# The gates' stage taken into the recurrent mixer's stage

## What is computed

```python
h = h + _L0_attn_ref(_layernorm(h), W_qkv, conv_w, W_z, W_b, W_a, dt_bias, A_log, ...)
# inside it
mixed = hidden_states @ W_qkv.T                      # 2048 channels
y = depthwise_conv(mixed, conv_w)                    # 4 taps along the sequence
mixed = silu(y)                                      # q, k: 8 heads of 64; v: 16 heads of 64
beta = sigmoid(hidden_states @ W_b.T)                # 16 gates
g = -exp(A_log) * softplus(hidden_states @ W_a.T + dt_bias)   # 16 decays
# then, row by row: S = S*exp(g); delta = (v - S k)*beta; S += k delta; o = S q
```

## Time and profile before

| | |
|---|---|
| median of 3 runs | 2748.21 us (2746.57 to 2750.3) |
| profiled execution | 2751.68 us, span 2750.0 us |
| mean granted TensorE clock | 0.924 |
| TensorE, VectorE, ScalarE, GpSimd busy over the span | 2363.9, 1981.4, 1304.2, 839.3 us |
| gates' stage | 671.8 to 736.2 |
| first pair's projection and convolution | 736.3 to 777.7 |
| first pair's own turn, up to the next pair's products | 777.7 to 832.4 |

### The profile page before, as it was taken

The page is one execution under the profiler, slowest core; times in us unless marked ns, Lnnn a source line. Parts: engine busy times, 40 slices in busy tenths (PEclk is TensorE's granted clock), DMA queues, the critical chain, the costliest instruction groups (busy, mean ns, idle before and its releaser), DMA issues. The chain is left out here.

```text
span 2750.0 us, 53589 instructions
## 1 busy us (share of the span) xinstructions
PE 2363.9 (86%) x19286; PEld 1813.9 (66%) x19286; DVE 1981.4 (72%) x4757; ACT 1304.2 (47%) x3127; POOL 839.3 (31%) x698
## 2 busy tenths in 40 slices
PE   7999998997747998889899989878487958799998
PEld 6777776885725777777777777756374845577654
DVE  4898984333368898988888888897755436787772
ACT  0444443211256777767676777774130214455232
POOL 2111100000113333333333333334876037560110
PEclk9999998998568999999999999998778977899999
DMA  4221001001412221111122222233221862220000
GB/s 158 75 76 29 14 10 51 23 24 44 156 24 51 54 53 46 45 49 50 41 51 53 52 56 55 55 82 83 77 46 25 295 188 75 73 62 1 8 21 28
DMA packets 274614, 169.24 MB, mean 62 GB/s; under 512 B 182863, under 2 KB 250590, under 8 KB 274000
## 3 DMA queue, kind: packets, MB, share of 16 engines
q1 hardware_dynamic: 248221, 140.55, 18.0%
q0 software_dynamic: 26112, 25.03, 3.5%
HBM read 99.49 MB, written 73.45 MB: 63 GB/s over the span
## 5 line engine op out<-in xcount | busy, mean ns | idle before, releaser
L1405 POOL TENSOR_TENSOR qd<-decay,qm 114x456 f32<-114x456 f32 x128 | 162.0, 1285 | 551.8 <-DVE qm L1604 464.3
L2358 PEld LDWEIGHTS d_ps<-d_xT,resid 128*128 128x128 f32 x1024 | 198.0, 195 | 47.1 <-issue 29.7
L2358 PE MATMUL d_ps<-d_xT,resid 128*128 128x228 f32 x1024 | 216.5, 363 | 12.3 <-DMA d_xT<-normed_t 12.3
L1585 DVE TENSOR_TENSOR ue<-ue,elim_tmp 128x30 f32<-128x30 f32 (+14 forms) x480 | 210.2, 438 | 16.8
L3028 POOL DMA_INDIRECT s_eo<-rows_y,slots_all x128 | 153.2, 1197 | 147.4 <-POOLq L2795 109.4
L1583 DVE TENSOR_TENSOR elim_tmp<-ue 128x30 f32<-128x30 f32 (+14 forms) x480 | 178.6, 372 | 25.2 <-issue 9.8
L1647 DVE SCALAR_TENSOR_TENSOR y_v<-raw,taps,y_v 128x228 f32<-128x228 f32 x384 | 163.4, 498 | 45.0 <-ACT y_v L2025 45.0
L1987 ACT ACTIVATE decay<-d_ps,gates 114x114 f32<-114x114 f32 x512 | 137.9, 362 | 83.7 <-DVE nt L1617 48.6
L1647 DVE SCALAR_TENSOR_TENSOR y_qk<-raw,taps,y_qk 128x228 f32<-128x228 f32 x384 | 146.5, 455 | 23.3 <-ACT y_qk L2025 23.3
L1998 ACT ACTIVATE gl<-upto,gates 114x114 f32<-114x114 f32 x512 | 156.1, 392 | 0.5 <-PE d_ps L2346 0.2
L2334 PE MATMUL d_ps<-y_qk 64*114 64x228 f32 x512 | 73.8, 411 | 95.6 <-DVE nt L1617 57.0
(11 more groups left out here) (370 smaller groups left out, 5698.9 us busy)
## 6 DMA issues: line engine op xcount, KB each, us to landing
rows_x<-zero_row SPq DMA_DIRECT2D x4, 2048.0 KB
ue<-blocks_n SPq DMA_DIRECT2D x16, 512.0 KB, 5.1
blocks_u<-ue SPq DMA_DIRECT2D x16, 512.0 KB, 3.0
blocks_v<-on SPq DMA_DIRECT2D x16, 512.0 KB, 3.1
e_x<-rows_x SPq DMA_DIRECT2D x32, 256.0 KB, 4.5
e_gu<-L_ffn_w_gate_up SPq DMA_DIRECT2D x32, 256.0 KB, 4.6
rows_y<-e_y SPq DMA_DIRECT2D x32, 256.0 KB, 3.8
blocks_n<-nt SPq DMA_DIRECT2D x96, 64.0 KB
```

What stands on the lines that cost most here:

```text
L1405: pool.tensor_tensor(qd[p.par][s][:, hs(u), :].rearrange("p (a o b) t -> p a o b t", o=2, b=2)[:, :, o], e[o][:, :, :].rearrange("p (a b) ...
L1585: step = dve.tensor_tensor(ue[:, 0:j, j + 1:], ue[:, 0:j, j + 1:], part, ALU.subtract)
L2358: last = pe.matmul(ps[:, f % 2, (t % 2) * W:(t % 2 + 1) * W], w_qkv[:, k, t * 128:(t + 1) * 128], xT[:, k, :], start=(k == 0), stop=(k == ...
```

## The change

`prepare` is removed as a stage and its work moves into the block of `delta_net`, with `first_turns`. The group's functions (statistics, scaling, gate read, turn, gate product, copy, store) stay as they were; their buffers are now tiles of the mixer that are not yet in use (`upd` and `sz` for the four loads, `qd1` for the scaled rows, `on` for the columns, `nt1` for the softplus), and their banks are 2 to 5 for the turns and 6 and 7 for the gate products, so that banks 0 and 1 are free for projections.

The first pair (`p`) is projected and convolved between the groups, each engine's order written out by hand. SP loads the mixer's weights ahead of every store and of the loads of groups 4 to 7, and the first pair's columns once the store of group 0 has landed. The tile of gates is finished in two halves of 16 samples: the first after group 3's gate read, the second inside the first pair's own turn. VectorE's statistics, power and scaling of a group follow each other directly. The first pair's turn is that of `iteration(Pair(0, 0))`, with the second half of the gates put in.

Cut to its core:

```diff
-def prepare(c, hid, xts, gates, w_qkv, taps, qmask):
...
-c.stage(prepare, hid, xts, gates, w_qkv, taps, qmask)
...
-def first_turns(iteration, between=None):
-
-iteration(Pair(0, -1), a=False, z=False, d=False)
-if between:
-    between()
-iteration(Pair(0, 0), z=False, d=False)
-iteration(Pair(0, 1), d=False)
-iteration(Pair(0, 2))
-iteration(Pair(0, 3))
 
...
+    load_group(0)
...
+    for g in range(1, GB):
+        load_group(g)
+    sp.dma_start(w_qkv[:, :, :], dr["L0_attn_W_qkv_t"].rearrange("(k p) n -> p k n", p=128)).then_inc(mix_in, 16)
+    sp.dma_start(taps[:, :, :], dr["L0_attn_conv_w_c"]).then_inc(mix_in, 16)
+    c.clear_old(sp)
+    store_group(0)
+    load_group(4)
+    store_group(1)
+    load_group(5)
+    sp.wait_ge(xT_out[0], 16)
     load_x(Pair(0, 0))
+    store_group(2)
+    load_group(6)
+    store_group(3)
+    load_group(7)
     sp.dma_start(nd.rearrange("s h q j i -> (s h q) (j i)").rearrange("p (a d) -> p a d", d=D),
                  c.zero_row[:, :].unsqueeze(1).to_broadcast([128, 4, D])).then_inc(nd_zero, 16)
     sp.dma_start(w_z[:, :, :], dr["L0_attn_W_z_t"].rearrange("(k p) n -> p k n", p=128)).then_inc(wz_in, 16)
+    for g in range(FIRST, GROUPS):
+        store_group(g)
+    iteration(Pair(0, -1), a=False, z=False, d=False)
...
+    pool.memset(raw[:, :, :, 0:TAPS - 1], 0.0).then_inc(d_init, 1)
+    group_power(0)
+    group_power(1)
+    group_power(2)
+    group_power(3)
+    for s in range(2):
+        pool.memset(ut[s][:, :, :], 0.0).then_inc(d_init, 1)
+        pool.memset(zs[s][:, :, :], 0.0).then_inc(d_init, 1)
+    group_power(4)
...
+    def coefficients():
+        ch.note(dve.tensor_scalar(qmask[:, :], c.upto[:, :], -DH ** -0.5, None, ALU.mult))
+        dve.wait_ge(g_coef, 1)
+        ch.note(dve.tensor_scalar(coef[:, 0:H], coef[:, 0:H], -1.0, None, ALU.mult))
+        ch.note(dve.memset(coef[:, H:], -1.0))
+        ch.sync()
+    def positive(q):
+        dve.wait_ge(g_abs, q + 1)
+        ch(dve.tensor_scalar(gates[:, g_half(q), :], gates[:, g_half(q), :], 0.0, None, ALU.max))
+    def log_gates(q):
+        half = gates[:, g_half(q), :]
+        dve.wait_ge(g_exp, 2 * q + 2)
+        ch(dve.tensor_tensor(half, half, g_soft[:, g_half(q), :], ALU.add))
+        ch(dve.tensor_tensor(half, half, coef[:, :].unsqueeze(1).to_broadcast([S, B // 2, 2 * H]), ALU.mult))
+        dve.tensor_scalar(half, half, LOG_ZERO, None, ALU.max).then_inc(gates_r, 1)
+    p, nxt = Pair(0, 0), Pair(0, 1)
+    stat(0)
+    scale(0)
+    stat(1)
+    scale(1)
+    stat(2)
+    scale(2)
+    gate_read(0)
+    stat(3)
+    scale(3)
+    gate_read(1)
+    stat(4)
+    gate_read(2)
+    scale(4)
+    dve.wait_ge(mix_in, 32)
+    dve.tensor_scalar(taps[:, :, :], taps[:, :, :], 0.5, None, ALU.mult).then_inc(taps_r, 1)
+    dve.wait_ge(taps_r, 1)
+    gate_read(3)
+    coefficients()
+    positive(0)
+    stat(5)
+    scale(5)
+    conv(p, 0, 1)
+    conv(p, 0, 2)
+    conv(p, 0, 3)
+    log_gates(0)
+    gate_read(4)
+    stat(6)
+    scale(6)
+    conv(p, 1, 1)
+    conv(p, 1, 2)
+    conv(p, 1, 3)
+    gate_read(5)
+    stat(7)
+    scale(7)
+    conv(p, 2, 1)
+    conv(p, 2, 2)
+    conv(p, 2, 3)
+    gate_read(6)
+    silu(p, 0)
+    conv(p, 3, 1)
+    conv(p, 3, 2)
+    conv(p, 3, 3)
+    gate_read(7)
+    silu(p, 1)
+    ch.end()
+    scale_gate()
+    query_mask(p, 0)
+    weights(p, 0)
+    weights(p, 1)
+    query_mask(p, 1)
+    weights(p, 2)
+    weights(p, 3)
+    weights(p, 4)
+    query_mask(p, 2)
+    weights(p, 5)
+    query_mask(p, 3)
+    positive(1)
+    conv(nxt, 0, 1)
+    conv(nxt, 0, 2)
+    conv(nxt, 0, 3)
+    weights(p, 6)
+    weights(p, 7)
+    conv(nxt, 1, 1)
+    conv(nxt, 1, 2)
+    conv(nxt, 1, 3)
+    conv(nxt, 2, 1)
+    conv(nxt, 2, 2)
+    conv(nxt, 2, 3)
+    log_gates(1)
+    conv(nxt, 3, 1)
+    conv(nxt, 3, 2)
+    conv(nxt, 3, 3)
+    silu(nxt, 0)
+    silu(nxt, 1)
+    ch.end()
+    for n in range(2):
+        dve.wait_ge(xT_out[n], 16 * (GROUPS // 2))
...
+    def softplus(q):
+        soft = g_soft[:, g_half(q), :]
+        act.wait_ge(ab_read, 2 * GROUPS // 2 * (q + 1))
+        act.activation(soft, gates[:, g_half(q), :], ACT.Abs).then_inc(g_abs, 1)
+        act.wait_ge(g_abs, q + 1)
+        act.activation(soft, soft, ACT.Exp, scale=-1.0).then_inc(g_exp, 1)
+        act.wait_ge(g_exp, 2 * q + 1)
+        act.activation(soft, soft, ACT.Ln, bias=1.0).then_inc(g_exp, 1)
+    p, nxt = Pair(0, 0), Pair(0, 1)
+    group_read(0)
+    group_read(1)
+    act.wait_ge(gw_in, 64)
+    act.activation(coef[:, 0:H], coef[:, 0:H], ACT.Exp).then_inc(g_coef, 1)
+    group_read(2)
+    group_read(3)
+    raw_read(p, 0)
+    raw_read(p, 1)
+    act.wait_ge(taps_r, 1)
+    softplus(0)
+    group_read(4)
+    raw_read(p, 2)
+    raw_read(p, 3)
+    first_tap(p, 0)
+    raw_read(p, 4)
+    raw_read(p, 5)
+    group_read(5)
+    first_tap(p, 1)
+    raw_read(p, 6)
+    raw_read(p, 7)
+    group_read(6)
+    first_tap(p, 2)
+    first_tap(p, 3)
+    tanh(p, 0)
+    act.wait_ge(gates_r, 1)
+    decay_terms(p, 0)
+    group_read(7)
+    decay_terms(p, 1)
+    tanh(p, 1)
+    decay_exp(p, 0)
+    decay_terms(p, 2)
+    decay_exp(p, 1)
+    decay_terms(p, 3)
+    raw_read(nxt, 0)
+    raw_read(nxt, 1)
+    raw_read(nxt, 2)
+    raw_read(nxt, 3)
+    raw_read(nxt, 4)
+    decay_exp(p, 2)
+    raw_read(nxt, 5)
+    raw_read(nxt, 6)
+    decay_terms(p, 4)
+    decay_exp(p, 3)
+    raw_read(nxt, 7)
+    decay_terms(p, 5)
+    decay_exp(p, 4)
+    decay_terms(p, 6)
+    decay_terms(p, 7)
+    decay_exp(p, 5)
+    softplus(1)
+    decay_terms(nxt, 0)
+    first_tap(nxt, 0)
+    first_tap(nxt, 1)
+    decay_exp(p, 6)
+    decay_exp(p, 7)
+    first_tap(nxt, 2)
+    first_tap(nxt, 3)
+    tanh(nxt, 0)
+    tanh(nxt, 1)
+    decay_terms(nxt, 1)
+    act.wait_ge(gates_r, 2)
...
+    p, nxt = Pair(0, 0), Pair(0, 1)
+    turn_group(0)
+    turn_group(1)
+    group_gates(0)
+    turn_group(2)
+    group_gates(1)
+    turn_group(3)
+    group_gates(2)
+    pe.wait_ge(mix_in, 32)
+    project(p, 0)
+    project(p, 1)
+    group_gates(3)
+    turn_group(4)
+    project(p, 2)
+    project(p, 3)
+    turn_group(5)
+    group_gates(4)
+    project(p, 4)
+    project(p, 5)
+    turn_group(6)
+    group_gates(5)
+    project(p, 6)
+    project(p, 7)
+    turn_group(7)
+    group_gates(6)
+    group_gates(7)
+    decay(p, 0)
+    products(p, 0)
+    decay(p, 1)
+    project(nxt, 0)
...
```

More of the change, by code:

```diff
@@ new lines, in scale @@
+                def scale(g):
+                    dve.wait_ge(grstd, g + 1)
+                    if g >= 2:
+                        dve.wait_ge(g_t, 2 * (g - 1))
+                    for s in range(GS):
+                        last = dve.tensor_scalar(g_xn[g % 2][:, s, :], g_hs[g % GB][:, s, :], g_mv[g % 2][:, s, 0:1],
+                                                 g_rstd[g % 2][:, s:s + 1], ALU.subtract, ALU.mult)
+                        if s < GS - 1:
+                            ch.note(last)
+                    ch.sync()
+                    last.then_inc(gxn, 1)
@@ L1971, in _ @@
+                iteration(Pair(0, 3))
                 with dve.Fori(0, LOOPS) as j:
@@ L2761, in last_turns, with turn_group @@
                         down(g)
-                first_turns(iteration)
+                def turn_group(g):
+                    pe.wait_ge(gxn, g + 1)
+                    if g >= 2:
+                        pe.wait_ge(gxT, g - 1)
+                    bank = 2 + 2 * (g % 2)
+                    for k in range(KD):
+                        for s in range(GS):
+                            last = pe.transpose(ps[:, bank + k, s * S:(s + 1) * S], g_xn[g % 2][:, s, k * 128:(k + 1) * 128],
+                                                c.ident[0:S, 0:S])
+                        last.then_inc(g_t, 1)
@@ new lines, in group_gates @@
+                def group_gates(g):
+                    if g == 0:
+                        pe.wait_ge(gw_in, 64)
+                    pe.wait_ge(gxT, g + 1)
+                    if g >= 2:
+                        pe.wait_ge(ab_read, 2 * (g - 1))
+                    for s in range(GS):
+                        for k in range(KD):
+                            last = pe.matmul(ps[0:S, 6 + g % 2, s * 2 * H:(s + 1) * 2 * H], g_xT[g % 2][:, k, s * S:(s + 1) * S],
+                                             w_ab[:, k, :], start=(k == 0), stop=(k == KD - 1))
+                    last.then_inc(ab_mm, 1)
@@ new lines, in _ @@
+                project(nxt, 3)
+                project(nxt, 4)
+                decay(p, 3)
+                project(nxt, 5)
+                products(p, 1)
+                project(nxt, 6)
+                decay(p, 4)
+                project(nxt, 7)
+                decay(p, 5)
+                products(p, 2)
+                decay(p, 6)
+                products(p, 3)
+                decay(p, 7)
+                iteration(Pair(0, 1), d=False)
+                iteration(Pair(0, 2))
+                iteration(Pair(0, 3))
```

248 lines of the change are left out of this document (87 added, 161 removed).

## The result

| | before | changed |
|---|---|---|
| median, measured together | 2749.75 us (2746.57 to 2753.1, 5 runs) | 2734.46 us (2731.95 to 2736.64, 5 runs) |
| the same pair measured again later | 2753.69 us (2747.32 to 2754.6, 9 runs) | 2729.3 us (2727.97 to 2739.54, 5 runs) |
| profiled execution, span | 2750.0 us | 2733.0 us |

The account below looks back on a forecast made before the run. Bound: two stretches in sequence, 106 us with 53.5 us of work on the busiest engine, refilled as load queue and engine orders allow. Gain 17.6 (middle of 20.3 and 14.9) less 1.0, taken as 16: 2732 us, range 2722 to 2745.

Parts of the forecast that it names:

- Step 1, the queue: Load queue ahead of the first projection: 6.07 MB at 177 GB/s, first pair's columns landing at 707, bounds 701 to 714.
- Step 2: Up to the first half of the gates: two projections done at 713, group 3's gate product at 714.6 to 716.1.
- The new order's worst stall: VectorE, idle since about 707, waits some 8 us to read group 3's gates, which stands in front of group 5's statistics.
- Steps 3 and 4: First pair and hand-over: first products at 756 or 762, second pair's first raw read at 763.2 or 768.6, gain 20.3 or 14.9.
- the high column: Timetable with TensorE's clock high for the middle pairs of projections: first tile 726.8, silus 752.4 and 760.8; low: 729.9, 757.9, 766.2.
- Step 5: Gates' second half inside the first pair's turn, covered by VectorE's wait for GpSimd's mask: costs 1 us, 3.4 without that cover.
- the prediction's own sign: Step 5 is wrong if VectorE does not wait for the mask, or second pair's first taps slip by over 2 us.
- Nothing downstream should give the gain back.: Behind the second pair's turn the kernel is unchanged and each turn follows the one before, so the gain should stay.
- (a): Rival: overlap mostly in name, first columns land behind the last group at 716 to 718; gain 6, 2742 us; chance 0.09.
- (b): Rival: TensorE's clock stays low through the first pair's turn too, costing 8.4 us of 14; 2743 us; chance 0.11.
- (d): Rival: slower, first columns land late, at 737 behind 9.4 MB at the lowest queue rate; 2762 us; chance 0.06.
- (c): Rival: hand-overs hide, weights at 304 GB/s, columns at 703, clock high in all pairs; gain some 24, 2724 us; chance 0.06.

## Why the prediction came out

The number was right: 16 us forecast, 15.3 and 24.4 between the medians, 19.0 at the first elimination. Step by step:

- **Step 1, the queue.** Columns at 707 forecast, in use at 708.58: right within its bounds. The copy on the chip confirms that this landing held the first projection (2.9 us).
- **Step 2.** Gate read of group 3 at 714.6 to 716.1 behind a stall of some 8 us: 716.25, 8.67 us. Place and size right. "The new order's worst stall" was wrong in weight: with the stall cut to 1.96 us the raw read moved by 1.0.
- **Steps 3 and 4.** First products at 756 or 762: 757.58. First raw read at 763.2 or 768.6: 763.37, the gain of 20.3 rather than the middle taken. VectorE met the high column within 1 us (first tile done at 727.7 for 726.8, first silu at 753.0 for 752.4, second at 761.3 for 760.8), yet the clock was not high in every pair: the four pairs of projections took 6.04, 3.26, 6.20 and 4.72 us at granted clocks of 0.54, 1.00, 0.53 and 0.70. In the second profile of the change the third pair took 4.64, and the raw read came no earlier (91.6 against 91.4). So the clock did not choose between the columns, as the prediction had it.
- **Step 5.** One microsecond forecast; 20.3 became 19.0, and leaving the half out gave 1.2 back. Size right, mechanism not: the sum took the 2.67 us of waiting for the mask as a cover that stays. The mask moved instead: 10.07 us became 3.24, and VectorE's own end decides; by the prediction's own sign the step was wrong. The first taps slipped by 1.2 us against the turn (from 24.8 to 26.1 us behind the raw read), where 1.8 was forecast. On the table loads the row held: in the change the load for the logarithm starts at 718.01 and takes 1.28, the function starts at 719.31.

```profile
718.01 1.28 ACT L2355 ACT_TABLE_LOAD   x1
719.31 0.63 ACT L2355 ACTIVATE nt<-nt 114x512 f32<-114x512 f32 x1
```

The Trainium skill's 2.66 us for a switch (ScalarE: Activation LUTs, What ACT_TABLE_LOAD costs) shows in no row here.
- **"Nothing downstream should give the gain back."** Not settled. The changed kernel's way is 2 to 7 us longer than that of the kernel before in the profiles, yet its two measurements, 15 and 24 us, lie on both sides of the 19.0.
- **What failed is the reading of where the room comes from.** The prediction set 106 us of elapsed time against 53.5 us of work and took the filling of one stage's gaps with the other's work for the gain. The walk of the new order was right as a timetable, but no rival asked what the same merge gives with the pair behind the groups. It gives all of it: 9.7 us from the border (TensorE's wait of 12.26 us there) and about as much from first taps behind two raw reads instead of eight. Starting the pair 22 us earlier bought nothing while each pair of projections waited between groups; it paid only where the first projections fill TensorE's idle time ahead of group 3's turn and of the landing (7.4 us). So the number is no test of the reason given for it: the walk summed the waits of the new order, whichever edit had removed the old ones.

Of the rivals, (a) was right that the overlap earns nothing and wrong in why (the columns were in time) and in the price. (b)'s low clock did not last, (d)'s late columns did not come; (c)'s 24 us is what the second measurement gave, but not by (c)'s way: the columns were in use at 708.58, not at 703.

## What to carry to other kernels

When a change bundles a merge, an interleave and rewritten orders, walk the version without its headline part as well: a timetable that ends at the right time doesn't tell which edit earns it. An early start is worth what the last engine in the chain ends earlier, so look for the consumer that waits for a whole batch (here first taps behind eight raw reads) before weaving two stages together. Don't book a wait for another engine as cover without asking what makes that engine late.

## What was not expected of the hardware

GpSimd's mask over 128 x 1024 has two lengths in the first pair's turn: 10.06 to 10.22 us in the five profiles in which VectorE's convolutions and silus run beside it without a gap, and 2.54 to 3.24 in the nine in which the gates' logarithm stands between them; there two of VectorE's three operations took 1.63 and 1.38 us instead of 0.69 and 0.43. The long ones all end 1.1 us behind VectorE's last silu, so most of the 10 us is probably waiting. VectorE's scaling of a group took 4.76 to 5.13 us beside GpSimd's clears, in the nine profiles of merged stages that have them there, and 1.38 without. The Trainium skill (SBUF — State Buffer, SBUF: two separate sides) says that the two engines share a pair of ports, which one of them holds for a whole instruction while the other is blocked, where VectorE's operation runs in a two-port mode, or has two SBUF inputs and GpSimd's operation reads SBUF. The lengths agree with that in kind; the long masks overlap 16 or 17 instructions of VectorE, not one, and no run here took the ports apart from the rest.
